# Plain fp32 products from raw operands in place of three products of rounded halves, in the four-layer network and in both expert layers

## The reference, cut to what matters

```python
# layer 0: the four-layer network (each _tlin is x @ w.T * s)
h = silu(_tlin(x, w1_w, w1_s)) * _tlin(x, w2_w, w2_s)      # 128 -> 512, twice
h = gelu(_tlin(h, h1_w, h1_s), approximate=False)          # 512 -> 512
h = gelu(_tlin(h, h2_w, h2_s), approximate=False)          # 512 -> 512
return _tlin(h, w3_w, w3_s)                                # 512 -> 128
# layer 1: 8 experts, F = 256, the gates keep the best 2
hid = silu(einsum('td,edf->tef', t, w1)) * einsum('td,edf->tef', t, w3)
y_e = einsum('tef,efd->ted', hid, w2)
y = einsum('ted,te->td', y_e, gate)
# layer 2: 8 experts, DF = 512, the gates keep the best 2
h = gelu(einsum('td,efd->tef', xf, W1) + b1, approximate=False)
y = einsum('tef,edf->ted', h, W2) + b2
out = einsum('ted,te->td', y, w)
```

## Time and profile before

| | us |
|---|---|
| median of 3 executions | 2379.31 (2364.61 to 2383.41) |
| the profiled execution | 2380.9, its span 2379.1 |
| PE busy | 2093.7 (88%), 15206 matmul records |
| DVE busy | 1531.5 (64%) |
| ACT busy | 1066.7 (45%) |
| POOL busy | 606.8 (26%) |
| mean granted TensorE clock | 0.902 |

### The profile page before, as it was taken

How to read it: one execution, slowest core, us unless ns; L and a number is a source line. 1 busy time by engine, 2 the same in 40 slices (tenths; PEclk the granted TensorE clock), 3 DMA queues, 4 the chain that set the end, 5 groups by cost and what they waited for, 6 DMA issues and landing times. The chain is left out here.

```text
span 2379.1 us, 40889 instructions
## 1 busy us (share of the span) xinstructions
PE 2093.7 (88%) x15206; PEld 1293.5 (54%) x15206; DVE 1531.5 (64%) x4178; ACT 1066.7 (45%) x1905; POOL 606.8 (26%) x867
## 2 busy tenths in 40 slices
PE   3688889998588888799999999988899999999993
PEld 1455556676476666455654556544554555555552
DVE  5677665432577776577747766557855677776655
ACT  2344533332355556244543434424354556555542
POOL 3421002001422221232202322243301233433232
PEclk9888889999789999799999999985569999999995
DMA  7556300300455554121200200016520000000001
GB/s 191 108 124 125 65 1 15 57 1 1 82 93 104 105 103 111 36 53 42 57 16 1 45 1 1 1 60 142 128 57 25 10 10 10 9 10 10 10 1 36
DMA packets 153138, 121.94 MB, mean 51 GB/s; under 512 B 21980, under 2 KB 145828, under 8 KB 147236
## 3 DMA queue, kind: packets, MB, share of 16 engines
q1 hardware_dynamic: 152940, 119.32, 23.0%
HBM read 78.04 MB, written 39.85 MB: 50 GB/s over the span
## 5 line engine op out<-in xcount | busy, mean ns | idle before, releaser
L1841 DVE TENSOR_REDUCE mneg<-psb 128x4 f32<-128x512 f32 (+1 forms) x576 | 388.7, 685 | 168.4 <-PE psb L1441 165.8
L2139 ACT ACTIVATE HB<-psb 128x512 f32<-128x512 f32 x384 | 226.7, 598 | 203.7 <-PE psb L1441 200.7
L1441 PE MATMUL psb<-K,Q 96*128 96x128 bf16 x1280 | 192.4, 256 | 54.7 <-DVE mneg L1841 32.7
L1440 PE MATMUL psb<-HB,KS 128*128 128x512 f32 x512 | 232.9, 598 | 0.0
L1441 PE MATMUL psb<-Q,K 99*128 99x128 bf16 x1280 | 150.3, 251 | 79.6 <-DMA Q<-mT 79.4
L1982 DVE TENSOR_TENSOR OE<-psb,OE 128x512 f32<-128x512 f32 x120 | 82.7, 689 | 191.1 <-ACT OE L2211 190.4
L2321 POOL TENSOR_SCALAR rs<-mv 128x2 f32<-128x2 f32 (+1 forms) x104 | 24.0, 230 | 712.0 <-DVE mv L1799 704.0
L2211 ACT ACTIVATE OE<-psb 128x512 f32<-128x512 f32 x128 | 76.5, 597 | 287.6 <-PE psb L1440 287.3
L2139 ACT ACTIVATE HB<-psb,bias 128x512 f32<-128x512 f32 x192 | 131.9, 687 | 145.4 <-PE psb L1441 143.8
L2207 ACT ACTIVATE HB<-psb,cols 128x512 f32<-128x512 f32 x256 | 171.3, 690 | 44.5 <-PE psb L1440 43.2
L1441 PEld LDWEIGHTS psb<-K,Q 96*128 96x128 bf16 x1280 | 112.1, 113 | 132.3 <-issue 61.5
(11 more groups left out here) (347 smaller groups left out, 4637.4 us busy)
## 6 DMA issues: line engine op xcount, KB each, us to landing
K<-sc_k SPq DMA_DIRECT2D x32, 384.0 KB, 5.0
Q<-sc_q SPq DMA_DIRECT2D x32, 384.0 KB
sc_q<-comp SPq DMA_DIRECT2D x48, 192.0 KB, 2.3
sc_q<-comp SPq DMA_DIRECT2D x48, 128.0 KB, 2.1
vraw<-in_ctx SPq DMA_DIRECT2D x48, 128.0 KB, 6.9
KS<-sc_s SPq DMA_DIRECT2D x16, 384.0 KB
K<-sc_k SPq DMA_DIRECT2D x32, 192.0 KB, 3.6
Q<-sc_q SPq DMA_DIRECT2D x32, 192.0 KB, 4.4
```

The source lines that it names most:

```text
L1440: return pe.e.matmul(out, w, x, start=start, stop=stop)
L1441: return pe.e.matmul(out, w, x, start=start, stop=stop, skip_group_check=True)
L1841: t = e.tensor_reduce(m.mneg[:, s.b % 4, s.i * A.per:(s.i + 1) * A.per], PSB[s.use.bank].rearrange("p (h k) -> p h k", h=A.per), AX.X, ALU ...
L2139: a.done(act(m.HB[:, s.slot, :], PSB[s.use.bank], ACT.Exp, bias=bz), s.use.drained)
```

## The change

`product`, `halves` and all the fp32r tiles are gone. `f0_mix`, `m1_up` and `m2_up` read the raw tiles, and each product is one fp32 matmul in all groups. What the products wait for is now the raw activation itself (`ub.drained`, `u.drained`, `tt_done`) and the load of the weights. Nothing else is put elsewhere: the streams of ACT, POOL and SP hold the same instructions in the same order, and DVE's stream is the one of before less its 208 instructions of `halves`. TensorE's loses three matmuls per product and gains one, 704 times.

```diff
-    def halves(hi, lo, raw, *need):
-        t = inc("dve", "halved")
-        do("halves", hi=hi, lo=lo, raw=raw, need=need, done=t)
-        return t
...
     def ffn0():
...
-                hid[g].append(halves(("first", m), ("rest", k, m), ("space", k, m), ub.drained, fr["first"], now0))
+                hid[g].append(ub.drained)
...
-                do("f0_mix1", k=k, m=m, use=u, parts=tuple(need), weight=t_h1, free=(fr["hB"], start_w[0]))
-                hid[g].append(halves(("UR", 4 + m), ("HBr", 4 + m), ("HB", 4 + m), u.drained, fr["hB"]))
+                do("f0_mix1", k=k, m=m, use=u, parts=tuple(need), weight=t_w["big"], free=(fr["hB"], start_w[0]))
+                hid[g].append(u.drained)
...
-                do("f0_mix2", k=k, m=m, use=u, parts=tuple(need), weight=t_h2, free=(hA_free[k], start_w[k]))
+                do("f0_mix2", k=k, m=m, use=u, parts=tuple(need), weight=t_w["big"], free=(hA_free[k], start_w[k]))
...
         n_(0)
         t_(0)
-        t_h1 = halves(("h1", 0), ("h1", 1), ("w", "h1T"), now0, t_w["big"])
         n_(1)
         up(0)
         t_(1)
-        t_h2 = halves(("h2", 0), ("h2", 1), ("w", "h2T"), now0, t_w["big"])
         mix1(0)
...
     def each1(n):
-        if 1 <= n <= 8:
-            for o in (256 * (n - 1), 2048 + 256 * (n - 1)):
-                half1["w", n - 1] = halves(("KFr", o, 256), ("WBr", o, 256), ("WB", o, 256), used1[n - 1])
-        if n % 8 == 5 and n // 8 + 1 < NG:
-            g = n // 8 + 1
-            half1["x", g] = halves(("KFr", 5120 + 512 * (g % 2), 512), ("CFr", 512 * g, 512), ("CF", 512 * g, 512),
-                                   tt_done[g], tt_read[g], half1.get(("free", g % 2)))
...
     def each2(n):
...
-        for ex, at_ in ((0, 2), (1, 3), (2, 4), (3, 5), (7, 9), (4, 10), (5, 11), (6, 12)):
-            if n == at_:
-                halves2(ex)
-        if n % 8 == 5 and n // 8 + 1 < NG:
-            g = n // 8 + 1
-            half2["x", g] = halves(("xnr", g % 2), ("WBr", 512 * g, 512), ("WB", 512 * g, 512), tt_done[g], tt_read[g], half2["free", g % 2])
...
-    def product(out, w, x, start=True, stop=True):
-
-        matmul(out, w[0], x[0], start, False)
-        matmul(out, w[0], x[1], False, False)
-        return matmul(out, w[1], x[0], False, stop)
...
-            t = product(PSB[s.use.bank], (w[0][:, o], w[1][:, o]), (hi(c), lo(c)), c == 0, c == 3)
+            t = matmul(PSB[s.use.bank], w[:, o], x[:, c, :], c == 0, c == 3)
...
     def m1_up(s):
...
-            x = m.KFr[:, 5120 + 512 * (s.g % 2):5632 + 512 * (s.g % 2)], m.CFr[:, 512 * s.g:512 * s.g + 512]
-            pe.done(product(PSB[s.ua.bank], (m.KFr[:, o:o + 128], m.WBr[:, o:o + 128]), x), s.ua.full)
-            pe.wait_ge(s.ub.before)
-            pe.done(product(PSB[s.ub.bank], (m.KFr[:, o2:o2 + 128], m.WBr[:, o2:o2 + 128]), x), s.ub.full)
+        x = m.TT[:, 512 * s.g:512 * s.g + 512]
+        pe.done(matmul(PSB[s.ua.bank], m.WB[:, o:o + 128], x, True, True), s.ua.full)
+        pe.wait_ge(s.ub.before)
+        pe.done(matmul(PSB[s.ub.bank], m.WB[:, o2:o2 + 128], x, True, True), s.ub.full)
...
     def m2_up(s):
...
-            t = product(PSB[s.use.bank], (m.hi2(s.ex)[:, 128 * s.c:128 * s.c + 128], m.w1(o, m.KFr, m.QFr)),
-                        (m.xnr[:, s.g % 2, :], m.WBr[:, 512 * s.g:512 * s.g + 512]))
-        pe.done(t, s.use.full)
+        pe.done(matmul(PSB[s.use.bank], m.w1(o, m.KF, m.QF), m.T2[:, 512 * s.g:512 * s.g + 512], True, True), s.use.full)
...
-    def halves(s):
-        hi, lo, raw = view(m, s.hi), view(m, s.lo), view(m, s.raw)
-        v.wait_ge(s.need)
-        v.wait_ge(v.step(e.tensor_copy(hi, raw)))
-        v.done(e.tensor_tensor(lo, raw, hi.bitcast(F32), ALU.subtract), s.done)
```

More of the change, by code:

```diff
@@ L159, in __init__ @@
         self.X = sb("X", [128, B, D])
[L160 to L165, removed]
         self.U = sb("U", [128, B, D])
@@ L779, in ffn0 @@
         hA_free = [None, None]
-        fr = {"hB": None, "first": None, "nf": None, "tf": None}
+        fr = {"hB": None, "nf": None, "tf": None}
         xt, nt, hid, yt = {}, {}, {}, {}
@@ L809, in mix1 @@
                 u = use(bank(), "act")
-                do("f0_mix1", k=k, m=m, use=u, parts=tuple(need), weight=t_h1, free=(fr["hB"], start_w[0]))
-                hid[g].append(halves(("UR", 4 + m), ("HBr", 4 + m), ("HB", 4 + m), u.drained, fr["hB"]))
+                do("f0_mix1", k=k, m=m, use=u, parts=tuple(need), weight=t_w["big"], free=(fr["hB"], start_w[0]))
+                hid[g].append(u.drained)
                 slot_no[0] += 4
                 run_side(1)
-            hA_free[k] = fr["first"] = u.full
+            hA_free[k] = u.full
         def mix2(g):
@@ L1092, in up1 @@
             ua, ub = use(bank(), "act"), use(bank(), "dve")
-            need = (t_m, tt_done[g]) if g == 0 else (half1["x", g], half1["w", ex])
+            need = t_m, tt_done[g]
             do("m1_up", g=g, ex=ex, c=c, slot=slots[c], ua=ua, ub=ub, need=need, at_free=at_free[c], h_free=chunk_free[slots[c]])
[L1095 to L1098, removed]
             at_free[c] = ub.drained
@@ L1149, in init2 @@
         return u.drained
-    used2, half2 = {}, {}
     L3 = {}
[L1154 to L1157, removed]
     def up2(g, ex):
@@ L1163, in up2 @@
             u = use(bank(), "act")
-            need = (t_w1[ex // 4], tt_done[g]) if g == 0 else (half2["x", g], half2["w", ex])
+            need = t_w1[ex // 4], tt_done[g]
             do("m2_up", g=g, ex=ex, c=c, slot=slots[c], use=u, need=need, h_free=chunk_free[slots[c]])
[L1166 to L1169, removed]
             th.append(u.drained)
@@ L1354, in make_plan @@
     fr["xf"] = fr["gate"] = now()
-    half2["now"], half2["free", 0], half2["free", 1] = now(), now(), now()
     own3 = {}
@@ L1384, in view @@
 def view(m, what):
-    name, i, *rest = what if isinstance(what, tuple) else (what, 0)
-    n = rest[0] if rest else 512
-    if name in ("WBr", "CFr", "KFr", "QFr"):
-        return {"WBr": m.WBr, "CFr": m.CFr, "KFr": m.KFr, "QFr": m.QFr}[name][:, i:i + n]
-    if name in ("WB", "CF", "KF", "QF"):
-        return {"WB": m.WB, "CF": m.CF, "KF": m.KF, "QF": m.QF}[name][:, i:i + n]
+    name, i = what
     if name in ("sp32", "xT"):
@@ L1395, in view @@
         return m.AT[:, 1, 0:256]
-    if name == "first":
-        return m.first[i]
-    if name == "rest":
-        return m.rest[i][:, n, :]
-    if name == "space":
-        return m.space[i][:, n, :]
-    if name in ("UR", "HBr", "HB"):
-        return {"UR": m.UR, "HBr": m.HBr, "HB": m.HB}[name][:, i, :]
-    if name in ("h1", "h2"):
-        return (m.h1 if name == "h1" else m.h2)[i]
-    if name == "w":
-        return m.wb[i]
-    if name == "hi2":
-        return m.hi2(i)
-    if name == "xnr":
-        return m.xnr[:, i, :]
 def x_front(m, xf):
@@ L1557, in f0_mix @@
             pe.wait_ge(s.parts[c])
[L1558 removed]
+            t = matmul(PSB[s.use.bank], w[:, o], x[:, c, :], c == 0, c == 3)
         pe.done(t, s.use.full)
     def f0_mix1(s):
[L1562 removed]
+        f0_mix(s, m.wb["h1T"], m.space[s.k])
     def f0_mix2(s):
[L1565 removed]
+        f0_mix(s, m.wb["h2T"], m.HB[:, 4:8, :])
     def f0_down(s):
@@ L1613, in m1_up @@
         pe.wait_ge(s.need, s.ua.before)
-        if s.g == 0:
-            x = m.TT[:, 0:512]
-            pe.done(matmul(PSB[s.ua.bank], m.WB[:, o:o + 128], x, True, True), s.ua.full)
-            pe.wait_ge(s.ub.before)
-            pe.done(matmul(PSB[s.ub.bank], m.WB[:, o2:o2 + 128], x, True, True), s.ub.full)
-        else:
-            x = m.KFr[:, 5120 + 512 * (s.g % 2):5632 + 512 * (s.g % 2)], m.CFr[:, 512 * s.g:512 * s.g + 512]
-            pe.done(product(PSB[s.ua.bank], (m.KFr[:, o:o + 128], m.WBr[:, o:o + 128]), x), s.ua.full)
-            pe.wait_ge(s.ub.before)
-            pe.done(product(PSB[s.ub.bank], (m.KFr[:, o2:o2 + 128], m.WBr[:, o2:o2 + 128]), x), s.ub.full)
+        x = m.TT[:, 512 * s.g:512 * s.g + 512]
+        pe.done(matmul(PSB[s.ua.bank], m.WB[:, o:o + 128], x, True, True), s.ua.full)
+        pe.wait_ge(s.ub.before)
+        pe.done(matmul(PSB[s.ub.bank], m.WB[:, o2:o2 + 128], x, True, True), s.ub.full)
     def m2_up(s):
@@ L1627, in m2_up @@
         pe.wait_ge(s.need, s.use.before)
-        if s.g == 0:
-            t = matmul(PSB[s.use.bank], m.w1(o, m.KF, m.QF), m.T2[:, 0:512], True, True)
-        else:
-            t = product(PSB[s.use.bank], (m.hi2(s.ex)[:, 128 * s.c:128 * s.c + 128], m.w1(o, m.KFr, m.QFr)),
-                        (m.xnr[:, s.g % 2, :], m.WBr[:, 512 * s.g:512 * s.g + 512]))
-        pe.done(t, s.use.full)
+        pe.done(matmul(PSB[s.use.bank], m.w1(o, m.KF, m.QF), m.T2[:, 512 * s.g:512 * s.g + 512], True, True), s.use.full)
     def moe_back(s):
```

21 lines of the change are left out of this document (3 added, 18 removed).

## The result

| | before | changed |
|---|---|---|
| median of 4 executions, us | 2379.64 (2364.61 to 2383.41) | 2466.74 (2466.45 to 2471.54) |
| ratio, 95% interval | | 1.0383 (1.0337 to 1.0429) |
| profiled execution, its span, us | 2380.9, 2379.1 | 2471.54, 2469.8 |
| DVE busy, us | 1531.5 | 1406.1 |

A forecast was written before the change was run, and what follows sets the result against it. The prediction took PE's matmul time to bound the network and both expert layers; +42, +35 and +32 us summed to +109, giving 2488 us, with a range of 2460 to 2510.

The forecast's parts named there:

- PE bounds the three stages: Network and both expert layers: PE's queue of matmuls sets the end; a plain product is 0.175 us dearer on PE.
- The four passes of the Trainium skill: All 704 products: at the fp32r price per pass, a plain product would take 0.91 us, adding 160 us; chance 0.03.
- The network, +42: Four-layer network: 64 output blocks, each 0.70 us longer, give +44.8 us, less what comes back at the start.
- The relief at the start: Network's start: DVE no longer spends 3.5 us halving h1; 2.5 us taken back, bounds 0 and 3.5.
- The halvings beside the path: Network: activation halvings on DVE, 0.43 + 0.69 us each, lie beside PE, so removing them is worth nothing.
- The waits that shrink: Expert layers: PE's waits shrink as its queue lengthens; 2 us taken back in the first, 5 in the second.
- one wait row at 3.4 us: First expert layer: waits on DVE's product of silu and up (L1973), 3.4 us in the whole stage.
- the bound of 13.5: Second expert layer: PE's waits for ACT's and DVE's results of layer 3's chain, 13.5 us from 1900 to 2320.
- Rival 1: Expert layers: PE's slack takes more, all waits go at 0.59 us per expert; +90, so 2470 us; chance 0.12.
- All lower bounds of the forecast together: Forecast's own range, low side: price per expert -8, the start -1, the waits -10 us.
- Rival 2: Untouched stage's clock: attention of layer 2 at full clock, -30, 2459 us, chance 0.08; another stage slower, +25, 2513, chance 0.05.

## Why the prediction was right, and where it was off

- **PE bounds the three stages, and a plain product costs 0.855 us against three times 0.227.** Right. The network gives 0.176 us per product where 0.175 was forecast, six of eight experts give 0.63 to 0.69 where 0.66 was taken, and leaving one matmul out or adding one moves the network's groups by the same 0.227 us.
- **The four passes of the Trainium skill** ("FP8 and Floating Point Precision", section "TensorE Precision Notes"). The number of passes is not contradicted: four fp32r matmuls and one plain product lie 6% apart. The step from passes to 160 us was wrong by the price of a pass: each fp32r matmul here costs 0.227, a quarter of a plain product 0.214.
- **The network, +42.** Right, +43.0: eight groups of 5.62 are 45.0, less 2.0. The relief at the start was taken as 2.5 us; 1.3 of it are the halvings', since the stage is that much longer where they are kept.
- **The halvings beside the path are worth nothing.** Right in all steady groups, shown from both sides. DVE's busy time fell by 125.4 us, as forecast. They were not nothing outside them: 1.5 us in group 0 of experts 1 and some 2 us in groups 1 and 6 of experts 2, for which the sum had no term.
- **The waits that shrink** are the terms that were mis-sized: 2 us taken in the first expert layer, 5 in the second. At 0.685 us for each of 56 experts the first would cost 38.4 and cost 29.6, so 9 went; in the second 0.65 x 56 = 36.4 against 19.6, so 17 went. For the first I had bounded the term by one wait row at 3.4 us. The same view of the kernel before has another, which the prediction left out:

```profile
PE psb L1440 <- DVE OE L1982: 2.6, 4, 0.7
```

Both are gone in the changed kernel: 6.0 us. The other 3 are what such rows cannot show: they count only the time in which no modelled matmul was under way, and in the fourth group they show 0.64 and 0.41 us where the distances between gate matmuls show 1.6. By the distances the 9 us are 1.5 in group 0, 1.0 in group 1 and 1.6 in each of groups 2 to 5. By cause, 4.5 are the table loads and 1.5 the halvings of group 0; the rest is not shown by a run. In the second layer 17 is more even than the bound of 13.5, because 4.8 of it are the clock (3.2 by the luck of the two traces, 1.6 where a wait is covered) and some 2 are DVE's halvings. The sum had neither. Rival 1 had the right mechanism and, at 2470 us, nearly the right time; but it priced an expert at 0.59 us, lower than what was measured, and let all 13.5 us of waits go where some stayed, so its nearness is no proof of its sum. All lower bounds of the forecast together (-8, -1 and -10) give 2469, still above the 2467 measured; the range of 2460 to 2510 held because it was widened to take in the rivals.
- **The clock.** Rival 2's stage did move, by 4.8 us, and it moves as much where nothing ahead of it was changed. That the clock could move inside the second expert layer, which the stretch of rows 2 shows at 1.00, was not thought of; there it makes another 4.8 us between the two traces.

## What to carry to other kernels

Price a change of matmuls by distances between starts, and look for the same work done both ways in one trace: group 0 was a finished experiment. Then lay the distances of a whole period side by side and find the places that are longer than their work, since those absorb added work and give nothing back for removed work; the rows of waits understate them. Do this for every group and not for one: where one expert is much longer than its like, look at its granted clock. And before choosing between exact products, look at the values: weights without low parts need two matmuls, which gained 3% where the change lost 4.

## What the runs showed of the hardware

- A plain fp32 product of 128x512 stands in the trace as two records, 0.43 us each from start to start at the full clock; an fp32r matmul takes 0.227. Four fp32r matmuls cost 0.051 us more than one plain product.
- A change between silu and gelu or exp costs ACT 1.28 us each way. In a stage that ACT does not bound, two of them per group still cost PE 1.2 us of 43.5. A version with eight or so per group was 9 us slower than the one with two; the link to the table loads was not tried by itself.
- The attention of layer 2 takes 170 to 182 us in traces of different kernels with the same instructions there; in the two stretches shown the mean granted clock is 0.66 and 0.55.
- After a wait of 2.0 us in one expert of the second layer the granted clock can fall or not, with the same instructions: 10.78 us at a mean of 0.84 and 9.15 at 1.00.
